# One block for the first self-attention and the sign MLP, and an earlier place for the weights' expansion in VectorE's turn

## What is computed

```python
x = x + _L0_attn_ref(_layernorm(x), ...)     # 16 heads of 32; q and k both pass a 32x32 matrix Wp
x = x + _L0_ffn_ref(_layernorm(x), k0, k1, k2, s0, s1, s2)

def _conn_dense(kernel_bool, x):
    w = jnp.where(kernel_bool, jnp.float32(1.0), jnp.float32(-1.0))
    return x @ w
h = jnp.concatenate([x, -x], axis=-1)
h = s0 * _conn_dense(k0, h)                  # k0: 1024 x 2048 bits
h = jax.nn.relu(h) * 2
h = s1 * _conn_dense(k1, h)                  # k1: 2048 x 2048 bits
h = jax.nn.relu(h) * 2
h = s2 * _conn_dense(k2, h)                  # k2: 2048 x 512 bits
```

## Time and profile before

| | |
|---|---|
| median of 3 runs | 1227.01 us (1225.33 to 1227.49) |
| profiled execution | 1233.02 us, span 1231.2 us |
| TensorE busy | 1115.7 us, 91% |
| VectorE, ScalarE, GpSimd busy | 574.8, 378.0, 187.2 us |
| mean granted TensorE clock | 0.96 |
| self-attention, first to last instruction of VectorE | 179.85 to 319.45 us |
| first matmul of the sign MLP | 321.00 us |

### The profile page before, as it was taken

How to read it: one execution, slowest core, us unless ns; L and a number is a source line. 1 busy time by engine, 2 the same in 40 slices (tenths; PEclk the granted TensorE clock), 3 DMA queues, 4 the chain that set the end, 5 groups by cost and what they waited for, 6 DMA issues and landing times. The chain is left out here.

```text
span 1231.2 us, 17899 instructions
## 1 busy us (share of the span) xinstructions
PE 1115.7 (91%) x6528; PEld 686.5 (56%) x6528; DVE 574.8 (47%) x998; ACT 378.0 (31%) x1012; POOL 187.2 (15%) x184
## 2 busy tenths in 40 slices
PE   8999979999799999999998999957899999994986
PEld 4544438877344444444443755437686867773542
DVE  2233026776652331511111544247848475668766
ACT  1211125665220100310100322233513233246873
POOL 0012001222122330000000112024213031300004
PEclk9999998999899999999999899979999999996999
DMA  9964702000111100000005777840000000007001
GB/s 339 387 251 169 264 3 76 2 1 1 52 26 43 34 17 1 0 1 0 0 0 207 267 267 271 327 145 26 1 1 0 0 0 0 0 0 282 1 1 68
DMA packets 55128, 108.61 MB, mean 88 GB/s; under 512 B 4144, under 2 KB 4528, under 8 KB 55088
## 3 DMA queue, kind: packets, MB, share of 16 engines
q1 hardware_dynamic: 55088, 108.09, 24.8%
HBM read 105.98 MB, written 2.10 MB: 88 GB/s over the span
## 5 line engine op out<-in xcount | busy, mean ns | idle before, releaser
L1643 ACT ACTIVATE f_act<-bank,f_sgn 128x512 f32<-128x512 f32 x64 | 44.0, 687 | 262.8 <-PE bank L1598 262.8
L1598 PE MATMUL bank<-f_a_hi,f_w 128*128 128x512 f16 x512 | 115.7, 379 | 0.0
L1598 PE MATMUL bank<-f_a_lo,f_w 128*128 128x512 f16 x512 | 115.7, 379 | 0.0
L1675 DVE CAST f_b_hi<-f_act 128x512 f32 x32 | 25.5, 797 | 166.2 <-ACT f_act L1643 166.2
L1598 PEld LDWEIGHTS bank<-f_a_lo,f_w 128*128 x512 | 50.1, 98 | 60.4
L1598 PEld LDWEIGHTS bank<-f_a_hi,f_w 128*128 x512 | 50.1, 98 | 60.2
L527 POOL TENSOR_TENSOR x_mv<-x_mv,eps 128x2 f32<-128x2 f32 x8 | 1.6, 195 | 402.8 <-DVE x_mv L420 402.8
L1448 DVE TENSOR_TENSOR s_e<-s_pair,s_tables 128x512 f32<-128x512 f32 x64 | 41.3, 687 | 42.1 <-POOL s_kT L1508 24.8
L276 PE MATMUL bank<-x_cT,x_qT 128*64 128x512 f32 x256 | 60.6, 620 | 0.0
L514 DVE TENSOR_TENSOR xres<-bank,xres 128x512 f32<-128x512 f32 (+1 forms) x16 | 11.1, 692 | 105.3 <-PE bank L333 91.5
L295 PE MATMUL bank<-x_cN,x_eT 128*64 128x512 f32 x256 | 58.4, 610 | 0.0
(11 more groups left out here) (315 smaller groups left out, 2278.4 us busy)
## 6 DMA issues: line engine op xcount, KB each, us to landing
x_cT<-in_ctx_cols_dram SPq DMA_DIRECT2D x32, 1024.0 KB, 7.6
x_cN<-in_ctx_rows_dram SPq DMA_DIRECT2D x32, 1024.0 KB, 9.8
f_upper_bits<-in_f_w_dram SPq DMA_DIRECT2D x20, 256.0 KB, 2.7
f_raw<-in_f_wd_dram SPq DMA_DIRECT2D x1, 2816.0 KB, 17.6
x_qw<-in_x_qw_dram SPq DMA_DIRECT2D x8, 256.0 KB, 4.2
x_kw<-in_x_kw_dram SPq DMA_DIRECT2D x8, 256.0 KB, 4.5
x_vw<-in_x_vw_dram SPq DMA_DIRECT2D x2, 1024.0 KB, 14.9
s_wk_ahead<-in_s_wk_dram SPq DMA_DIRECT2D x1, 2048.0 KB, 13.7
```

What stands on the lines that cost most here:

```text
L1598: mm = pe.matmul(h_bank[s][:, :], weights(2 * i + s, k), part[:, k, cols], start=(n == 0 and k == 0), stop=(n == 1 and k == k_chunks - 1))
L1643: act.activation(act32[s][:, :], h_bank[s][:, :], ACT.Relu, scale=sgn[:, layer % 2:layer % 2 + 1]).then_inc(h_read, 1)
L1675: dve.tensor_copy(hi[:, 2 * i + s, :], act32[s][:, :]).then_inc(hhi_ok, 1)
```

## The change

Both functions get a block from outside, the same one, so that no block ends between them, and the `end_phase()` between them is gone. The semaphores of both are cleared together after the MLP. SP's part of the MLP now begins with a wait for all four expansions, since its loads write into the space of `upper`. In VectorE's turn the expansion of the first weights moves ahead of the first maxima, and the maxima of tile 1's first group ahead of the subtraction for `f_xT_lo`.

```diff
-def head_attention(core, tag, heads, wq, ..., sign_weights, sign_inputs, sign_scales):
+def head_attention(core, block, tag, heads, wq, ..., sign_weights, sign_inputs, sign_scales):
...
         sc = sem("sign_scales_ok")
-        block = st.enter_context(nc.Block())
...
                 ins.then_inc(k1_ok, 1)
+                _, upper, lower, weights, _ = sign_weights
+                dve.wait_ge(bits_in, 32)
+                dve.tensor_tensor(weights[:, i, :], upper[:, i, :], lower[:, i, :], ALU.subtract).then_inc(sign_ok, 1)
                 negative_maxima(i, 0, 0)
                 negative_maxima(i, 0, 1)
                 if not last:
                     normalise_x(2 * i + 2, i + 1)
+                negative_maxima(i, 1, 0)
                 if not first:
                     for s in range(2):
                         at = bass.ts(2 * i + s - 2, P)
                         dve.wait_ge(fhi_ok, 2 * i + s - 1)
                         dve.tensor_tensor(fT_lo[:, :, at], as_chunks(bank[F_BANK[s]][:, :]), fT_hi[:, :, at],
                                           ALU.subtract).then_inc(flo_ok, 1)
-                negative_maxima(i, 1, 0)
                 negative_maxima(i, 1, 1)
-                _, upper, lower, weights, _ = sign_weights
-                dve.wait_ge(bits_in, 32)
-                dve.tensor_tensor(weights[:, i, :], upper[:, i, :], lower[:, i, :], ALU.subtract).then_inc(sign_ok, 1)
                 dve.wait_ge(v_done, 2 * i + 2)
...
             turn(3, False, True)
+        return sign_ok
...
-def sign_mlp(core, tag, w0_sb, bits, xT_hi, xT_lo, w1, w2, sgn, out_scale):
+def sign_mlp(core, block, tag, w0_sb, bits, xT_hi, xT_lo, w1, w2, sgn, out_scale, bits_read):
...
         y_read = sem("y_read")
-        block = st.enter_context(nc.Block())
         W2_RAW = HC * D // H
 
         @block.sync
         def _(sp):
+            sp.wait_ge(bits_read, KC)
             for n in range(HC):
...
         sign_stack = ExitStack()
+        phases = ExitStack()
...
-            head_attention(core, "s0", 16, ...)
+            block = phases.enter_context(nc.Block())
+            bits_read = head_attention(core, block, "s0", 16, ...)
-        core.end_phase()
-        sign_mlp(core, "f0", w0, upper, *sign_inputs, io["f0_w1"], io["f0_w2"], sgn, out_scale)
+        sign_mlp(core, block, "f0", w0, upper, *sign_inputs, io["f0_w1"], io["f0_w2"], sgn, out_scale, bits_read)
+        phases.close()
         sign_stack.close()
         core.end_phase()
```

More of the change, by code:

```diff
@@ L549, in _, with head_attention @@
             turn(TILES // 2 - 1, True)
-def head_attention(core, tag, heads, wq, wk, wv, bq, bk, bv, scale, wqT, wpT, ahead, sign_weights, sign_inputs, sign_scales):
+def head_attention(core, block, tag, heads, wq, wk, wv, bq, bk, bv, scale, wqT, wpT, ahead, sign_weights, sign_inputs, sign_scales):
     nc = core.nc
@@ L2113, in program @@
             lower = queries_weights.enter_context(nc.sbuf_tensor("f0_lower_bits", [P, KC, hidden], U8, side="right"))
-            head_attention(core, "s0", 16, io["s0_wq"], io["s0_wk"], io["s0_wv"], io["s0_bq"], io["s0_bk"], io["s0_bv"],
+            block = phases.enter_context(nc.Block())
+            bits_read = head_attention(core, block, "s0", 16, io["s0_wq"], io["s0_wk"], io["s0_wv"], io["s0_bq"], io["s0_bk"], io["s0_bv"],
                            32 ** -0.5, wqT, io["s0_wpT"], (held, on_chip), (io["f0_w0"], upper, lower, w0, io["f0_scales"]),
                            sign_inputs, (scales_in, sgn, out_scale))
-        core.end_phase()
-        sign_mlp(core, "f0", w0, upper, *sign_inputs, io["f0_w1"], io["f0_w2"], sgn, out_scale)
+        sign_mlp(core, block, "f0", w0, upper, *sign_inputs, io["f0_w1"], io["f0_w2"], sgn, out_scale, bits_read)
+        phases.close()
         sign_stack.close()
```

## The result

Over 20 executions each, the changed kernel has a median of 1225.93 us (1217.96 to 1227.90) and the kernel before 1228.05 (1225.33 to 1235.93). The ratio of their times is 0.9964, with a 95% interval of 0.9947 to 0.9980: 4.4 us faster, between 2.5 and 6.5. Put on the 1227.0 that the prediction starts from, that is 1222.6. The medians alone differ by only 2.1 and the means by 4.5. The times of both kernels fall into groups: seven of the changed kernel's lie between 1218.0 and 1222.7, thirteen between 1224.8 and 1227.9. Three executions in all that follows, two of c1 (1335 and 1740 us) and one of the kernel before (1334), ran at a mean granted clock of 0.83, 0.62 and 0.83, and the ratios leave them out.

What follows compares the result with a forecast made beforehand. The prediction took TensorE's idle time and low clock as the bound. Its terms, 3.28 - 0.2 + 2.47 + 1.0 = 6.55 us, took the median from 1227.0 to 1220.5 us, range 1218.2 to 1224.5.

Steps and rivals of the forecast that it cites:

- The copies behind the value projection: Copies into `s_v_diag` start right behind TensorE's value projection, shortening its waits in turns 1 to 3; 3.28 us together.
- Turn 0 at nothing: In turn 0 the copies wait for TensorE's value projection with or without the expansion in front; no gain.
- The port: VectorE's expansion and GpSimd's additions take turns at SBUF; first maxima 0.2 to 0.3 late in turn 1, 0.4 to 0.5 in turn 2.
- Turn 3 becomes like turn 2: In turn 3 the expansion would wait out GpSimd's running addition as in turn 2, making the first maxima similarly late.
- The 0.2 charged for ScalarE: Late first maxima delay ScalarE's exponentials; up to 0.2 us lost in turn 2, none in turns 1 and 3.
- The boundary: Between attention and MLP, the block end and meeting of engines go; 0.25 of VectorE's 1.24 us gap stays, 1.0 gained.
- TensorE's low clock at the MLP's start: At the MLP's start idle time falls from 5.5 to 4.5 us; clock left unchanged, bounds 0 to 1.5 us gained.
- The clock given back in turns 2 and 3: Shorter TensorE waits avoid the low clock behind them; 1.32 us in turn 2 and about 1.15 in turn 3, 2.47 together.
- the stretch shortens but the clock does not come back: Rival: waits and boundary gain 4.1 us, but turns 2 and 3 regain no clock; 1222.9 us, chance 0.18.
- Port kept: Rival: GpSimd holds the port for both additions, first maxima 1.6 to 1.7 us late in turns 1 and 2; 1225.8, chance 0.10.
- slower: Rival: VectorE held until GpSimd's whole string ends, first maxima 2.6 us late; 3.9 us slower, 1230.9, chance 0.06.
- Given back later: Rival: later stages, behind the boundary, get two more low clock stretches costing 2.6 us; 1223.1 or above, chance 0.11.

Runs made afterwards that it cites:

- c1: Changed kernel with GpSimd instead of VectorE raising the three counters that open the MLP, so TensorE starts it earlier; 1226.84 us, ratio 0.9966 to before.
- a2: Kernel before with VectorE's new order alone, keeping two blocks with the meeting between them; 1223.74 us, ratio 0.9963 to before.
- a4: Changed kernel with the expansion moved from ahead of the first maxima to behind the normalisation; 1225.50 us, ratio 0.9954 to before.
- b4: Changed kernel with the expansion run twice, the first time into a tensor nobody reads; 1231.26 us, ratio 1.0006 to before.
- a1: Changed kernel with VectorE's old order, so only the single block for both stages remains; 1226.51 us, ratio 0.9993 to before.
- b1: Changed kernel with 36 unread transposes of the identity between the attention's last matmul and the MLP's first; 1221.08 us, ratio 0.9924 to before.
- d3: Changed kernel with 18 unread transposes of the identity between the attention's last matmul and the MLP's first; 1220.96 us, ratio 0.9928 to before.
- a3: Kernel before with unread identity transposes filling TensorE's waits for the copied softmax weights in turns 1 to 3; 1230.24 us, ratio 1.0015 to before.
- d2: Changed kernel with GpSimd opening the MLP early, expansion behind the normalisation, and six hidden chunks split before the last normalisation; 1219.15 us, ratio 0.9914 to before.

## Why the prediction was right

The direction and the mechanism were right, point by point, and the size was too large: 6.5 us forecast, 4.4 measured.

- The copies behind the value projection, 1.14, 1.14 and 1.00: the waits changed by 1.14, 1.14 and 1.00 exactly. a2 shows that this comes from the order alone.
- Turn 0 at nothing: its wait stayed 0.89. VectorE now waits 2.24 us there for the value projection, and the expansion takes 2.28, so the old place was free in turn 0 and cost only later.
- The port: the expansion 0.2 and 1.0 longer than 2.28 in turns 1 and 2, maxima 0.12 and 0.27 late where I had 0.2 to 0.3 and 0.4 to 0.5. "Turn 3 becomes like turn 2" was wrong: there VectorE went first. The 0.2 charged for ScalarE measured 0.02. a4 and b4 show both sides of it: free on the path as it stands, and costly with a second expansion in front. At the MLP's start, too, GpSimd's first expansion now runs beside VectorE's two normalisations, which take 2.57 us for 1.00; from the MLP's first matmul on the profiles are equal, so this cost nothing.
- The Trainium skill's rule (page "SBUF — State Buffer", section "SBUF: two separate sides"), that of two such instructions the one that starts first keeps the other out for its whole length, agrees with both orders seen here: 3.27 us for VectorE in turn 2, behind GpSimd's first addition, and 4.54 for GpSimd's pair in turn 3, behind VectorE. Its warning decided nothing, for the stretch had room.
- The boundary, 1.0: 0.97 in the gap of VectorE, 1.08 in TensorE's idle time. The 0.9 timed in a1 agrees, but its interval includes zero.
- TensorE's low clock at the MLP's start, left as it is: it stayed, 0.50 over 315 to 321. 4.43 us of idle time brought it as 5.51 did; b1 and d3 show it gone with 0.35 and 2.31 left.
- The clock given back in turns 2 and 3, 2.47: this is the term that was mis-sized. "I take the new ones to be on the good side" held in the profile of the changed kernel, where the clock gave 2.6 and the stretch shrank by 6.98 where 6.55 was predicted. But I sized it from one execution in which the clock fell at two waits. a1's execution has it fall at one of the same two, and a3, which removes the idle time and moves nothing, was not faster.

How much of it the typical execution gets can be estimated, since every execution has a mean granted clock on record. Those of the changed kernel average 0.9629, the 76 of before beside the experiments 0.9618; 0.0011 of 1226 us is about 1.3 us, with an error of about the same size. At an equal mean clock of 0.962 seven executions of the changed kernel have a median of 1226.2 us and 21 of before one of 1229.5: 3.3 less, for the 4.1 of the terms without the clock (3.28 - 0.2 + 1.0). So 4.4 is some 3.3 from the waits and the boundary and some 1.1 from the clock, about half of what was forecast. Where in an execution its clock falls only the profiles show, so what turns 2 and 3 have of this stays open.

The rival "the stretch shortens but the clock does not come back", 4.1, is thus nearest to the time. The direction and most of the size come from the terms without the clock; the 6.5 itself lies at the end of the measured interval. "Port kept" and "slower" fell: the waiting VectorE operation went ahead of GpSimd's second addition in turns 1 and 2. "Given back later" fell in the profile: 910.2 us from the MLP's first matmul on, before and after. Its premise, that later stages differ from execution to execution, is right. From its first matmul to the rotary attention's first transposes the second cross attention, which no edit touches, takes 158.0 to 158.5 us in eight of the fourteen profiles, those of before and of the changed kernel among them, and 154.5 to 155.2 in the other six.

## What to carry to other kernels

An operation that nobody waits for still delays what stands behind it on its engine. Move it to where that engine waits anyway, here for TensorE's first scores, and look on the timeline for what other engines do then: here GpSimd's additions, which made the moved expansion up to 1.0 us longer. When one profile is all there is, count the clock given back by shorter idle times as a bound and not as a term, and compare the mean clock of many executions. The one long idle stretch ahead of a dense stage was worth filling; half of it was enough here, and it takes two lines. The early start alone only moved the wait; it paid once VectorE, which splits what TensorE has made, was freed as well.

## What was unexpected of the hardware

- The same idle time of 2.02 to 2.03 us in turn 2 was followed by a granted clock of 0.50 in the profile of before and by 1.00 in a1's.
- Executions of the same kernel differ in their mean granted clock, and the time follows: the changed kernel took 1227.5 to 1227.9 us at 0.961 and 1218.0 to 1221.6 at 0.965 to 0.968.
- 18 transposes of the identity, 2.18 us, at the head of an idle stretch of 4.5 kept the clock at 1.00 as well as 36 did, with 2.31 us idle behind them.
- Two VectorE normalisations of 0.5 us each took 4.15 with two GpSimd expansions of 128x2048 bytes beside them (c1), 2.57 with one (d3); a subtraction of 0.69 took 2.16 in d2.
